# The first 1024 rows of a four-layer graph kernel: centred on VectorE before they are turned, and the second half's turn moved behind the first sum tiles

## The reference, cut to what matters

```
h = max(layernorm(x), 0);  x = x + L0(h, adj)   # row-normalised adj @ h, @ W.T + b, ReLU
h = max(layernorm(x), 0);  x = x + L1(h, adj)   # two attention heads over N=4096, elu
h = max(layernorm(x), 0);  x = x + L2(h, adj)   # one attention head, ReLU
h = max(layernorm(x), 0);  x = x + L3(h, adj)   # adj.T @ h, divided by the column sums
layernorm(x) = (x - mean) / sqrt(var + 1e-5)
```

## Time and profile before

| | |
|---|---|
| median of 3 runs | 1193.92 us (1193.82 to 1194.11) |
| the profiled execution | 1193.39 us, its span 1191.6 us |
| TensorE busy | 1185.7 us (100% of the span) |
| VectorE busy | 938.3 us (79%) |
| ScalarE busy | 325.5 us (27%) |
| HBM read | 146.94 MB, 127 GB/s over the span |

### The profile page before, as it was taken

One profiled execution on the slowest core, in us unless ns is written; L12 is line 12 of the kernel. 1 busy time (PEld: TensorE's weight loads), 2 busy tenths in 40 slices (PEclk: granted clock), 3 DMA queues, 4 the chain that ended last, 5 costly groups with the idle time before them and its releaser, 6 DMA issues.

```text
span 1191.6 us, 16721 instructions
## 1 busy us (share of the span) xinstructions
PE 1185.7 (100%) x6235; PEld 816.7 (69%) x6235; DVE 938.3 (79%) x1677; ACT 325.5 (27%) x780; POOL 9.6 (1%) x20
## 2 busy tenths in 40 slices
PE   9999999999999999999999999999999999999999
PEld 9999999954444444444454547999999964444455
DVE  5548585798979787889797787788787869887786
ACT  4512122225323242423445234541212121000000
POOL 3000000000000000000000000000000000000000
DMA  9888898800111102110010101032303068999920
GB/s 324 304 279 291 248 347 305 282 29 15 40 18 37 18 35 35 53 18 22 1 22 0 40 1 40 1 108 90 141 0 141 1 268 304 313 329 322 322 82 18
DMA packets 90227, 156.30 MB, mean 131 GB/s; under 512 B 45904, under 2 KB 54448, under 8 KB 90160
## 3 DMA queue, kind: packets, MB, share of 16 engines
q1 hardware_dynamic: 64240, 148.58, 36.3%
q10 hardware_dynamic: 25456, 6.30, 2.4%
q0 software_dynamic: 464, 0.53, 0.2%
HBM read 146.94 MB, written 4.78 MB: 127 GB/s over the span
## 4 chain that ended last, share of the span: by engine, by line
PE 94%; DVE 4%; ACT 1%; DMA 0%; issue 0%; DVEq 0%; ACTq 0%
PE acc L555 48%; PE acc L539 36%; PE acc L802 4%; DVE ring L1367 2%; PE mix L621 1%; PE mix L593 1%; PE mix L608 1%; PE acc L810 1%; PE turn L570 1%; DMA ring<-in_adj_t 0%; DVE G L1367 0%; PE mix L670 0%; ACT V L829 0%; DVE stats L1170 0%; ACT U L829 0%
## 5 line engine op out<-in xcount | busy, mean ns | idle before, releaser
L1367 DVE SCALAR_TENSOR_TENSOR ring<-G,score,mask 128x1024 f32<-128x1024 f32 x372 | 466.8, 1280 | 70.9 <-PE acc L555 38.7
L555 PE MATMUL acc<-ring,G 128*128 128x512 f32 x1000 | 436.3, 593 | 0.3 <-DVE acc L1305 0.2
L555 PEld LDWEIGHTS acc<-ring,G 128*128 128x128 f32 x1000 | 186.5, 190 | 229.6 <-issue 210.9
L539 PE MATMUL acc<-G,ring 128*128 128x129 f32 x2240 | 253.9, 275 | 0.8 <-DVE acc L1316 0.7
L539 PEld LDWEIGHTS acc<-G,ring 128*128 128x128 f32 x2240 | 251.9, 192 | 2.1 <-DVE ring L1367 2.0
L539 PE MATMUL acc<-G,mask 128*128 128x129 f32 x1648 | 185.8, 275 | 0.0
L539 PEld LDWEIGHTS acc<-G,mask 128*128 128x128 f32 x1648 | 184.8, 192 | 0.0
L555 PE MATMUL acc<-mask,G 128*128 128x512 f32 x384 | 165.8, 593 | 0.0
L1637 DVE TENSOR_TENSOR ring<-ring,mask 128x1024 f32<-128x1024 f32 x120 | 146.8, 1223 | 11.0 <-DVE ring L1637 0.5
L555 PEld LDWEIGHTS acc<-mask,G 128*128 128x128 f32 x384 | 72.6, 190 | 91.0 <-issue 89.8
L1405 DVE TENSOR_SCALAR mask<-mask 128x1024 uint8<-128x1024 f32 x103 | 68.4, 689 | 27.4 <-DMA mask<-in_adj_t 26.8
(11 more groups left out here) (207 smaller groups left out, 707.0 us busy)
## 6 DMA issues: line engine op xcount, KB each, us to landing
mask<-in_adj SPq DMA_DIRECT2D x128, 512.0 KB, 5.5
mask<-in_adj_t SPq DMA_DIRECT2D x103, 512.0 KB, 5.2
ring<-in_adj_t SPq DMA_DIRECT2D x18, 512.0 KB, 6.4
G<-given_rows SPq DMA_DIRECT2D x10, 512.0 KB, 3.9
G<-in_adj_t SPq DMA_DIRECT2D x4, 512.0 KB, 6.4
G<-raw_rows SPq DMA_DIRECT2D x4, 512.0 KB, 5.2
inputs<-V ACTq DMA_DIRECT2D x4, 512.0 KB, 2.7
V<-inputs SPq DMA_DIRECT2D x4, 512.0 KB, 3.9
```

Source lines behind the costliest of these rows:

```text
L539: mm = pe.matmul(acc[:, b, (s % 3) * DW:(s % 3) * DW + DW], lhs[:, s * P:(s + 1) * P], g, start=(k == 0 and s % 3 == 0), stop=(k == T - 1) ...
L555: mm = pe.matmul(acc[:, c, :], g, moving[:, c * BANK:(c + 1) * BANK], start=(k == 0), stop=(k == T - 1), skip_group_check=True)
L1367: dve.scalar_tensor_tensor(slots[k % L], late_home[h] if early and k >= EARLY else rows_home[h, q], rank[h][:, k:k + 1], span(mask, (q * T ...
```

## The change

- The centring matrix and its two products go, with the semaphores centre_made and xt_kept.
- VectorE takes the statistics of one half, forms minus the mean, and writes max(x - mean, 0) of each of the four blocks into V with one operation each; then the variance of that half. It does so for both halves. The reciprocals stand between (half 0's behind the mean of half 1) and at the end (half 1's), ahead of the first mask.
- TensorE transposes V instead of X. The first half is turned and projected ahead of tile 0; the second half is turned behind tile 0 and projected behind tile 1.
- ScalarE copies each turned half to U, takes that half's square root, and places all eight blocks into G, four to a half. VectorE's multiplication for the second half goes.
- WARM is 9 instead of 7, and the warm-up reads block 7 of V, not block 0.
- f_var, f_dev and f_scale are counted once more than before, since the first quarter now raises each twice.

```diff
--- before.py
+++ after.py
@@ -85,7 +85,7 @@
     SPARE = 2
     BLOCKED = (2, 3)
     WEIGHTS = 14
-    WARM = 7
+    WARM = 9
 
     with ExitStack() as ctx:
         def sb(name, shape, dt=F32):
@@ -121,7 +121,6 @@
         inv = sb("inv", [P, S])
         zero = sb("zero", [P, S])
 
-        centre = ring[:, 0, 0:P]
         E = [ring[:, i, :] for i in range(EB)]
         spare = ring[:, 4, :]
         w0T = spare[:, 0:D]
@@ -145,6 +144,7 @@
         fold, later = [spare[:, o + 3 * D + i * S:o + 3 * D + (i + 1) * S] for i in range(2)]
         stream3 = mask[:, 0:DEEP * QC * 4].bitcast(F32).rearrange("p (s c) -> p s c", c=QC)
         stream0 = mask[:, (Q - 1) * T * QC:].bitcast(F32).rearrange("p (s c) -> p s c", c=QC)
+        halves_x = (slice(0, HALF), slice(HALF, S))
         U3 = U[:, :].rearrange("p (s d) -> p s d", d=DW)
         flat = U[:, 0:S * D]
         g1c, b1c, g2c, b2c, alphac, restc, top, bigc, wbias, vbias = [cols[:, i:i + 1] for i in range(10)]
@@ -190,8 +190,8 @@
 
 
         nothing_made = sem("nothing_made")
-        x_first, centre_made = sem("x_first"), sem("centre_made")
-        xt_kept, x_centred = sem("xt_kept"), sem("x_centred")
+        x_first = sem("x_first")
+        x_centred = sem("x_centred")
         x_loaded = [sem(f"x_loaded{q}") for q in range(Q)]
         w0_loaded, weights_loaded, w2_loaded = sem("w0_loaded"), sem("weights_loaded"), sem("w2_loaded")
         saved, back, stored = sem("saved"), sem("back"), sem("stored")
@@ -665,27 +665,26 @@
                         hooks[k]()
 
 
+            def turn_first(half):
+                pe.wait_ge(x_centred, half + 1)
+                for s in range(S)[halves_x[half]]:
+                    mm = pe.transpose(turn[:, s * P:(s + 1) * P], V[:, s, :], ident[:, :])
+                mm.then_inc(f_turned if half else h_turned, 1)
+
+            def project_first(half):
+                pe.wait_ge(f_wide if half else h_wide, 1)
+                for s in range(S)[halves_x[half]]:
+                    mm = pe.matmul(mixed[:, s * P:(s + 1) * P], U[:, s * P:(s + 1) * P], w0T, start=True, stop=True,
+                                   skip_group_check=True)
+                mm.then_inc(f_projected if half else h_projected, 1)
             pe.wait_ge(nothing_made, 1)
             for i in range(WARM):
-                pe.matmul(one, V[:, 0, :], V[:, 0, :], start=True, stop=True, skip_group_check=True)
+                pe.matmul(one, V[:, S - 1, :], V[:, S - 1, :], start=True, stop=True, skip_group_check=True)
             pe.wait_ge(consts_made, 2)
-            for half in range(2):
-                pe.wait_ge(x_loaded[0] if half else x_first, 16)
-                for s in range(half * HALF, (half + 1) * HALF):
-                    mm = pe.transpose(turn[:, s * P:(s + 1) * P], X[:, s, :], ident[:, :])
-                mm.then_inc(f_turned if half else h_turned, 1)
-            pe.wait_ge(centre_made, 1)
-            for half in range(2):
-                pe.wait_ge(xt_kept, half + 1)
-                pe.matmul(turn[:, half * BANK:(half + 1) * BANK], centre, U[:, half * BANK:(half + 1) * BANK],
-                          start=True, stop=True, skip_group_check=True).then_inc(x_centred, 1)
+            turn_first(0)
             pe.wait_ge(w0_loaded, 16)
             own = [feed(0, p, w0T, D, 0, 0) for p in range(Q)]
-            for half in range(2):
-                pe.wait_ge(f_wide if half else h_wide, 1)
-                for s in range(half * HALF, (half + 1) * HALF):
-                    mm = pe.matmul(mixed[:, s * P:(s + 1) * P], V[:, s, :], w0T, start=True, stop=True, skip_group_check=True)
-                mm.then_inc(f_projected if half else h_projected, 1)
+            project_first(0)
 
             def scores_behind_projections():
                 pe.wait_ge(weights_loaded, 16 * WEIGHTS)
@@ -694,7 +693,7 @@
                     mm = pe.matmul(one[:, 2 * h:2 * h + 2], raw, attnc[:, 2 * h:2 * h + 2], start=True, stop=True,
                                    skip_group_check=True)
                 mm.then_inc(qv_summed, 1)
-            run(0, 0, {5: own[1][0], 6: own[1][1], 14: own[2][1], 21: own[3][1], 28: scores_behind_projections})
+            run(0, 0, {0: lambda: turn_first(1), 1: lambda: project_first(1), 5: own[1][0], 6: own[1][1], 14: own[2][1], 21: own[3][1], 28: scores_behind_projections})
 
             def turn_weights_back():
 
@@ -867,21 +866,20 @@
 
             def first_rows():
 
-                for half in range(2):
+                for half, some in enumerate(halves_x):
                     act.wait_ge(f_turned if half else h_turned, 1)
-                    act.copy(U[:, half * BANK:(half + 1) * BANK], turn[:, half * BANK:(half + 1) * BANK]).then_inc(xt_kept, 1)
-                for half in range(2):
-                    act.wait_ge(x_centred, half + 1)
-                    act.activation(V[:, half * HALF:(half + 1) * HALF, :], turn[:, half * BANK:(half + 1) * BANK]
-                                   .rearrange("p (s d) -> p s d", d=D), ACT.Relu).then_inc(f_wide if half else h_wide, 1)
-                    if half == 0:
-                        deviation(f_var, 1, f_dev)
-                act.wait_ge(h_projected, 1)
-                act.wait_ge(f_scale, 1)
-                settle()
-                for s in range(HALF):
-                    act.activation(G[:, 0, s, 0:D], mixed3[:, s, :], ACT.Copy, scale=scale[:, s:s + 1])\
-                        .then_inc(h_placed if s < HALF - 1 else f_norm, 1)
+                    act.copy(U[:, half * BANK:(half + 1) * BANK], turn[:, half * BANK:(half + 1) * BANK])\
+                        .then_inc(f_wide if half else h_wide, 1)
+                    act.wait_ge(f_var, half + 1)
+                    act.activation(dev[:, some], var[:, some], ACT.Sqrt).then_inc(f_dev, 1)
+                    act.wait_ge(f_projected if half else h_projected, 1)
+                    act.wait_ge(f_scale, half + 1)
+                    settle()
+                    for s in range(S)[some]:
+                        ins = act.activation(G[:, 0, s, 0:D], mixed3[:, s, :], ACT.Copy, scale=scale[:, s:s + 1])
+                        if half == 0:
+                            ins.then_inc(h_placed if s < HALF - 1 else f_norm, 1)
+                ins.then_inc(f_placed, 1)
 
             def feed(h, p, q, between=()):
 
@@ -902,8 +900,8 @@
                     first_rows()
                     return
                 else:
-                    deviation(f_var, p - Q + 1 if h > 2 else p + 1, f_dev)
-                    act.wait_ge(f_scale, p - Q + 1 if h > 2 else p + 1)
+                    deviation(f_var, p - Q + 2 if h > 2 else p + 2, f_dev)
+                    act.wait_ge(f_scale, p - Q + 2 if h > 2 else p + 2)
                     settle()
                     if h == 4:
                         normalise(lambda s: blocks(G[:, 0, :, :], q, 1, s)[:, 0, 0:D], of_x, local(scale), local(shift),
@@ -1194,7 +1192,7 @@
 
             def feed(h, p, q):
 
-                c = p - Q + 1 if h > 2 else p + 1
+                c = p - Q + 2 if h > 2 else p + 2
 
                 def first_scales():
                     wait(dve, f_norm, p)
@@ -1372,24 +1370,39 @@
             def diagonal(q, s):
                 return span(mask, q * ((T + S) * QC) + s * (QC + P), P)
 
-            dve.memset(V[:, 0, :], 0.0).then_inc(nothing_made, 1)
+            dve.memset(V[:, S - 1, :], 0.0).then_inc(nothing_made, 1)
             for i in range(2):
                 dve.memset(G[:, i, :, D], 1.0)
             dve.memset(G[:, 1, :, D - 1], 1.0)
             st.mark(dve.memset(hmean, 0.0))
             own = [feed(0, p, p) for p in range(Q)]
-            dve.wait_ge(consts_made, 2)
-            dve.tensor_scalar(centre, ident[:, :], 1.0 / D, None, ALU.subtract).then_inc(centre_made, 1)
-            dve.wait_ge(x_first, 16)
-            own[0][0]()
-            dve.wait_ge(x_loaded[0], 16)
-            own[0][1]()
-            own[0][2]()
-
-            dve.wait_ge(f_scale, 1)
-            dve.wait_ge(f_projected, 1)
-            dve.tensor_tensor(G[:, 0, HALF:S, 0:D], mixed3[:, HALF:, :], scale[:, HALF:].unsqueeze(2).broadcast_to([P, HALF, D]),
-                              ALU.mult).then_inc(f_placed, 1)
+
+            def centre_first(half, between=()):
+                some = halves_x[half]
+                dve.wait_ge(x_loaded[0] if half else x_first, 16)
+                for s in range(S)[some]:
+                    ins = dve.bn_stats(stats[:, s, :], X[:, s, :])
+                st.then(ins)
+                st.then(dve.tensor_tensor(twice[:, some], stats[:, some, 1], stats[:, some, 4], ALU.add))
+                st.then(dve.tensor_scalar(mean[:, some], twice[:, some], -0.5, None, ALU.mult))
+                for step in between:
+                    step()
+                for s in range(S)[some]:
+                    ins = dve.tensor_scalar(V[:, s, :], X[:, s, :], mean[:, s:s + 1], 0.0, ALU.add, ALU.max)
```

(14 more changed lines are left out.)

## The result

The changed kernel took 1197.01 us (median of 20 runs, 1193.50 to 1199.28), the kernel before 1193.46 (20 runs, 1192.01 to 1194.65). The ratio is 1.0026, 95% interval 1.0019 to 1.0032. The forecast was 1194.7 with a range to 1196.3: the direction held, the size did not.

The account below looks back on a forecast made before the run. TensorE, busy 1185.7 of 1191.6 us, was taken as the bound: 1.33 us of work moved behind tile 0, less 0.55 us for its earlier start, gives +0.78 on 1193.92, so 1194.7 us; range 1193.4 to 1196.3.

Parts of the forecast that it names:

- the price of the order: TensorE's stream up to tile 6: 1.33 us moved behind tile 0, less 0.55 for its earlier start, +0.78 us.
- centring: VectorE's four centring operations on the first half, ahead of the transposes: 283 ns each, 0.88 us together.
- moved work: Second half's four transposes and four projections, now run after tiles 0 and 1 on TensorE: 1.33 us at full rate.
- The placing of the second half: ScalarE's four placings into G end about 15.5 us, covered by tiles 2 and 3: no cost.
- The masks: VectorE's first mask would start at about 12.9 us instead of 10.71, 2.2 us late.
- the wait for rows 1: TensorE waiting at about 21 us for VectorE's normalising of rows 1: slack 0.2 us, priced at nothing, up to 0.4.
- rival B: VectorE's lateness starves TensorE through the loads or rows 1: +0.2 to +1.5 us more, about 1195.5; 8 in 100.
- I put the rise at 6.1: TensorE's clock goes from its lower to its higher level at 6.1 us, ahead of tile 0.
- the 0.75 us of the transposes: First half's four transposes and ScalarE's wait for them, ahead of tile 0: 0.75 us at full rate, 1.31 at half.
- Rival A: TensorE's clock stays low: +2.3 us if it rises behind the first projections, +4.1 behind tile 0; 11 in 100.
- two more warm-up matmuls: Four more TensorE instructions at 0.24 us, ending about 5.4: delay nothing, and speak against the clock staying low.
- A's first part: TensorE's clock rises only behind the first projections: +2.3 us, 1196.2; 8 in 100.

Follow-up runs that it names:

- warm-up 11: The changed kernel with 11 warm-up matmuls instead of 9 and nothing else: 1194.58 us, +1.17 against the kernel before.
- later gaps filled: The changed kernel plus three idle matmuls behind the first four transposes and four behind the first projections, 9 warm-up matmuls kept: 1194.04 us, +0.58 against before.
- all gaps filled: The changed kernel with 11 warm-up matmuls, three idle matmuls behind the first transposes and four behind the first projections: 1194.73 us, +1.32 against before.
- second turn ahead: As all gaps filled, but the second half is transposed ahead of tile 0 in place of four idle matmuls: 1193.05 us, -0.36 against before.
- warm-up 7: The changed kernel with 7 warm-up matmuls instead of 9: 1196.72 us, +3.26 against the kernel before.

## Why the prediction was wrong

**Right: where to look, and the price of the order.** At the higher level TensorE's stream behaves as worked out: centring 0.87 to 0.89 for four (0.88), 279 ns each (283); moved work 1.33 (1.33); tile 6 at +0.70 with warm-up 11 (+0.78). The five runs of the lower cluster, +0.96, agree, and so do later gaps filled, warm-up 11 and all gaps filled, +0.58 to +1.32. The second turn ahead, -0.36, does not.

**Right as far as the traces show: what hides the rest.** The placing of the second half delayed nothing. The masks began at 12.44 with warm-up 11 (12.9) and at 16.1 in the profiled change, over 5 us late, and the span less tile 6 was 1170.9 against 1170.0, inside the 1168.8 to 1171.5 of all traces. TensorE has no idle time between tile 0 and 30 us in either trace of the change, so the wait for rows 1 at about 21 us, the sign of rival B, is not there. The second turn ahead leaves open whether late masks cost up to a microsecond elsewhere.

**Wrong: the step "I put the rise at 6.1" and with it the 0.75 us of the transposes.** For the kernel before the reading is right, its centring products run at the higher level. But I carried that moment over to a kernel that idles ahead of it. The full clock came at 16.54 us in one trace of the change and at about 13.5 in the other. The point depends on what TensorE did before, and it differs between executions. The sum then had the transposes, projections and tile 0 at 0.75 (0.63 in the chain), 1.14 and 1.79, where the two traces of the change have 1.10, 2.06, and 3.78 and 3.44. Rival A named this mechanism and priced it at +2.3 behind the first projections and +4.1 behind tile 0; the median fell between, at +3.55. What failed was its chance, 11 in 100. I let "two more warm-up matmuls" outweigh the three gaps I had listed myself, and took three runs within 0.29 us as a sign that the point does not vary. Twenty runs of before spread over 2.6 us. For a kernel without gaps a shift of the rise costs little (5.26 and about 6.1 us in its two traces, tile 0 at 9.78 and 9.83); its times say nothing for one with gaps. The rule of the Trainium skill cited with rival A ("TensorE: Matmul & The Clock Gate", "What's actually happening"), a release that varies from run to run, is borne out: those two points of one program, and two clusters of times. Two things stay open: why the rise waits when the idle stretches come, and whether in the runs with a mean granted clock of 0.997 the 7 us at the lower level lie ahead of a late rise or behind an early one, since none of them was profiled.

**Right by its sign only: the range.** It ended at 1196.3, just above A's first part. An honest weight on A would have taken it to 1198.

## What to carry to other kernels

Moving work behind the first bottleneck instruction gains only what that instruction starts earlier; the work itself is paid in full if the engine never waits again. Ahead of a long matmul stream count TensorE's idle stretches as well as its path: three of them, 2.2 us in all, went here with a late rise in most runs, which cost 2.8 us at tile 6 in one trace and 4.4 in the other, against the order's own 0.7. Read the level from the count or spacing of weight loads, in more than one execution, and look at the single times: the two clusters here were a switch, not noise.

## What the runs showed of the hardware that I had not expected

- The granted clock as the views print it reads 1.00 while TensorE runs at the lower of its two levels at the start (6 loads a microsecond against 11). The trace's clock records give the rise in 12 of 14 traces, in step with the spacing of the loads, and the mean granted clock of a run told in 16 of 28 long runs of the change and of its warm-up 7 (0.997), and in no other run.
- One program's rise moved between about 13.5 and 16.5 us, worth 1.54 us at tile 6. Once up, at 4.09 us, it was kept through 2.1 us of idle stretches of at most 0.8.
- The rest of the kernel varies by 2.7 us between executions (1168.8 to 1171.5), and goes with TensorE's few late waits: from 30 to 500 us it idled 0.3 us where the rest is 1168.8 and 2.1 where it is 1171.5. In the second trace of the kernel before, the new one is 0.8 us for a copy of quarter 2 (PE mix L593 <- ACT U L864), behind a late load of X. Its tile 0 starts at 9.78, before at 9.83, so these two executions of the kernel before differ in such waits and not in their beginning.
